# A fused attention, scan and MLP kernel: a chunk's normalisation chain queued later in stage 3, and half of an impulse response moved one step on

## The chip, the cores and the metric

The kernel runs on one core of a Trainium2 chip. The time is device microseconds of one execution, the median of three runs. A core has TensorE (PE), VectorE (DVE), ScalarE (ACT), GpSimd (POOL) and SyncE (SP), each with its own program; here SP issues all the DMA. The engines meet only at semaphores: an instruction waits until a semaphore has reached a count, and what stands behind it on its engine waits with it. All data are float32.

## The reference, cut to what matters

```python
# x: 128 batches x 32 tokens x 256;  ctx: 128 x 257 x 256
x = x + xattn(layernorm(x), ctx, w_sim, b_sim, W_qv, b_qv)

def attn(x, A, Bp, Cp, Dp, Wg, bg, gamma, beta):      # a gated linear scan over the 32 tokens
    xg = x * sigmoid(x @ Wg.T + bg)
    # s = s @ A + xt * Bp ;  y = s . Cp + Dp * xt   (per channel)
    y = scan(...) + xg
    return layernorm(y) * gamma + beta
x = x + attn(layernorm(x), ...)

def ffn(x, fast_b, w_fc, w_proj, u, v, gate):
    h = x @ (ternary(w_fc) * scale).T + gate * (x @ v.T @ fast_b.T @ u.T)
    r = maximum(h, 0)
    return (r * r) @ (ternary(w_proj) * scale).T      # hidden width 1024
x = x + ffn(layernorm(x), ...)
```

## The kernel before, in words

The 4096 tokens are 32 groups of 128. Stage 1 is a loop of 34 pipelined steps over the groups: in `step(g)` each engine works on the context of group g, the attention of g - 1 and the gate of g - 2. The scan is done as a convolution: every channel's impulse response over 32 tokens (`impulse`, from the state powers kept in `states`) is written to DRAM, read back as shifted windows, and placed in the matrix `toeplitz`, with which TensorE multiplies the gated tokens. The states are complete after step 28 (`LAST_STATE`); in step 29 GpSimd multiplies them by C, and VectorE sums them in two halves (`impulse_sums(0)`, `impulse_sums(1)`) and finishes with `impulse_response()`, which adds D and scales by 0.5. SP waits for that (`imp_steps`), stores the impulse, waits for the store and issues four loads of windows (`windows_load(q, 0)`); GpSimd and ScalarE place them from step 31 on.

In step 30 VectorE's order is: `bn_stats` of a coming group, x1 of group 28 (`resid` at L1500), the moments that `make_z` on ScalarE and `turn_z` on TensorE wait for, `normalise1(31)`, `hq`, `weights(30)` (a ternary pass), `dot1(31)` (L1413), then the products, `neg_max` and `zT_lo` (which TensorE's `sum_gate` waits for), and the softmax.

Stage 3 is the MLP over 8 chunks of 4 groups (512 tokens). A chunk c has 8 hidden tiles m. For each, TensorE makes `hidden_wide` (four matmuls, the high and low parts of xn against the ternary weights) and `hidden_low` (a fifth, the low-rank term), ScalarE a relu, VectorE the square, ScalarE its rounded high part `sq_hi`, GpSimd the rest `sq_lo`, and TensorE, three tiles behind, the projection: four matmuls with `sq_hi`, four with `sq_lo`. Two banks hold the hidden tiles, so a tile waits for the square two before it.

Before a chunk begins, its x must be made. With y the scan's output: sums and moments of y (`y_sums`, `y_moments`, DVE), the inverse deviation (`deviation_y`, `lower_y`, POOL), `norm_y` (ACT), `times_gamma` (POOL), `add_y` (DVE), and then the x chain: `x_sums`, `x_moments` (DVE), `deviation_x`, `lower_x` (POOL), `norm_x` (ACT), `turn_in` (PE transposes), `split_hi` (ACT), `split_lo` (DVE), `low_rank` (PE), `low_rank_hi` (ACT), `low_rank_parts` (DVE). Chunk 1 has a form of its own for the y part: `second_centre` and `second_add`, in halves. These steps are written by hand between the tiles of the chunks before: the loops over (c, m) of each engine say at which tile each step stands in that engine's queue. SP loads y of a chunk (`load_y`) when the adds before it are done (`x2_done`), which counts two for chunk 0 and one for each later chunk (`whole_chunks`).

## Time and profile before

| | us |
|---|---|
| three runs | 490.25, 490.37, 492.69 |
| median | 490.37 |
| profiled execution, its own time | 489.83 |
| its span, first to last instruction | 488.0 |
| PE busy | 467.5 (96%) |
| weight loads on PE | 403.8 (83%) |
| DVE busy | 398.0 (82%) |
| ACT busy | 361.5 (74%) |
| POOL busy | 340.3 (70%) |
| mean granted TensorE clock | 0.996 of full |

Stage 1 reaches to about 298 us of the span, the scan and the turning of the weights to about 326, and stage 3 from there to the end. A matmul's end is modelled and neighbours overlap, so a busy PE is not PE at its peak: from start to start is the better length. Idle time in brackets in a timeline is that of the engine ahead of the instruction, with what ended it. An engine that idles off the bound costs nothing.

### The profile page before, as it was taken

What the parts mean: (1) busy time and instruction counts of PE and PEld (TensorE: products, weight loads), DVE (VectorE), ACT (ScalarE), POOL (GpSimd) and SP (SyncE); (2) the same over time, 40 slices, a digit from 0 to 9 for tenths busy, and PEclk for the clock granted to TensorE, in tenths of its full rate; (3) what the DMA queues carried; (4) which work ended last, traced back from release to release, by engine and by line L of the source; (5) the groups of instructions that cost most, each with busy time, mean ns of one, the idle gap of its engine ahead of it and who ended that gap; (6) DMA issues with size and microseconds to landing.
All of it is one profiled execution on the core that took longest, in us unless ns stands there. A gap on an engine that the chain in (4) does not pass through costs nothing. (4 is left out here: it accounts for less than half of the span.)

```text
span 488.0 us, 13769 instructions
## 1 busy us (share of the span) xinstructions
PE 467.5 (96%) x4405; PEld 403.8 (83%) x4405; DVE 398.0 (82%) x1212; ACT 361.5 (74%) x880; POOL 340.3 (70%) x446
## 2 busy tenths in 40 slices
PE   8899999999999999999999898887999999999995
PEld 6688888989888898898988787776888888888885
DVE  2988888889889888899888876788769788797654
ACT  3787777878878878788787786656697786876752
POOL 2488997868667677776876766125789887887563
PEclk9999999999999999999999999999899999999999
DMA  7945647758757566674764747684021312301102
GB/s 258 316 151 161 217 155 195 223 155 241 184 148 229 145 194 186 164 218 140 230 171 142 192 120 164 144 259 130 0 57 32 87 43 45 87 6 39 44 1 88
DMA packets 77172, 70.29 MB, mean 144 GB/s; under 512 B 39319, under 2 KB 59948, under 8 KB 76588
## 3 DMA queue, kind: packets, MB, share of 16 engines
q1 hardware_dynamic: 77100, 69.41, 49.6%
q8 instruction: 36, 0.59, 0.5%
q14 instruction: 36, 0.29, 0.2%
HBM read 56.74 MB, written 12.65 MB: 142 GB/s over the span
## 5 line engine op out<-in xcount | busy, mean ns | idle before, releaser
L1958 POOL TENSOR_TENSOR sq_lo<-fc_in,sq_hi 128x512 fp32r<-128x512 f32 x63 | 82.7, 1315 | 29.3 <-ACT sq_hi L1909 29.3
L1041 ACT COPY ctxT<-turn_ps 128x512 f32<-128x512 f32 x128 | 68.9, 590 | 9.1 <-PE turn_ps L802 3.1
L1901 ACT ACTIVATE relu<-fc_ps,fc_square 128x512 f32<-128x512 f32 x64 | 43.8, 686 | 30.9 <-PE fc_ps L1820 30.8
L2003 DVE SCALAR_TENSOR_TENSOR fc_in<-fc_ps,relu 128x512 f32<-128x512 f32 x64 | 43.7, 685 | 26.4 <-ACT relu L1901 25.6
L1236 POOL TENSOR_TENSOR hb_lo<-hbT,hb_hi 128x256 fp32r<-128x256 f32 x32 | 23.9, 747 | 42.6 <-ACT hb_hi L1120 42.6
L1222 POOL TENSOR_TENSOR rstd<-ve,neg_half 128x1 f32<-128x1 f32 x64 | 35.1, 553 | 25.5 <-DVE ve L1511 18.4
L1814 PE MATMUL fc_ps<-xn_hi,fc_T 128*128 128x512 f32 x128 | 52.1, 407 | 0.5 <-DVE fc_in L2003 0.5
L1814 PE MATMUL fc_ps<-xn_lo,fc_T 128*128 128x512 f32 x128 | 50.9, 398 | 0.0
L1228 POOL TENSOR_TENSOR proj_in<-proj_in,below 128x512 f32<-128x512 f32 x31 | 48.1, 1552 | 0.0
L802 PE MATMUL turn_ps<-ident,ctxn 128*128 128x128 f32 x352 | 47.5, 278 | 0.0
L1837 PEld LDWEIGHTS proj_ps<-proj_T,sq_hi 128*128 128x128 f32 x252 | 38.8, 189 | 5.4
L1837 PE MATMUL proj_ps<-proj_T,sq_lo 128*128 128x256 f32 x252 | 40.2, 281 | 2.5 <-POOL sq_lo L1958 2.5
L802 PEld LDWEIGHTS turn_ps<-ident,ctxn 128*128 128x128 f32 x352 | 41.1, 147 | 0.4 <-ACT ctxT L1041 0.2
L1909 ACT CAST sq_hi<-fc_in 128x512 fp32r<-128x512 f32 x64 | 39.2, 613 | 1.9 <-DVE fc_in L2003 1.9
L1837 PE MATMUL proj_ps<-proj_T,sq_hi 128*128 128x256 f32 x252 | 40.3, 282 | 0.0
L1837 PEld LDWEIGHTS proj_ps<-proj_T,sq_lo 128*128 128x128 f32 x252 | 34.4, 188 | 2.7 <-POOL sq_lo L1958 2.7
L879 PE MATMUL score_ps<-ctxT,hcwT 128*32 128x257 f32 x512 | 33.7, 380 | 0.7 <-ACT ctxT L1041 0.7
L1814 PEld LDWEIGHTS fc_ps<-xn_hi,fc_T 128*128 128x128 f32 x128 | 24.3, 190 | 4.7 <-DVE fc_in L2003 1.3
L1048 ACT ACTIVATE xn<-resid,nmr,rstd 128x256 f32<-128x256 f32 x32 | 19.3, 603 | 11.0 <-DVE nmr L1456 10.8
L1072 ACT ACTIVATE hcwT<-hc_probT,w 128x128 f32<-128x128 f32 x62 | 27.3, 489 | 0.1
L1814 PEld LDWEIGHTS fc_ps<-xn_lo,fc_T 128*128 128x128 f32 x128 | 24.5, 191 | 3.3
L1236 POOL TENSOR_TENSOR hcq_lo<-y_in,hcq_hi 128x256 fp32r<-128x256 f32 x32 | 24.0, 751 | 4.0 <-ACT hcq_hi L1137 3.1
(261 smaller groups left out, 1449.5 us busy)
## 6 DMA issues: line engine op xcount, KB each, us to landing
ctxn<-in_ctx SPq DMA_DIRECT2D x22, 1024.0 KB, 5.5
toeplitz<-in_ctx SPq DMA_DIRECT2D x10, 1024.0 KB, 5.5
resid<-in_x SPq DMA_DIRECT2D x32, 128.0 KB, 5.4
ctx_end<-in_ctx SPq DMA_DIRECT2D x32, 128.0 KB
gated_tokens<-gated SPq DMA_DIRECT2D x32, 128.0 KB, 5.9
scan_x<-gated_tokens SPq DMA_DIRECT2D x60, 64.0 KB, 4.8
out<-resid SPq DMA_DIRECT2D x7, 512.0 KB, 3.2
scan_quarters<-scan_x SPq DMA_DIRECT2D x3, 1024.0 KB, 6.0
```

Source lines behind the costliest of these rows:

```text
L802: mm = pe.transpose(turn_ps[b % 2][:, (c * JT + t) * P:(c * JT + t + 1) * P], ctxn[g % DEEP][:, b, t, c * P:(c + 1) * P], ident[:, :])
L879: mm = pe.matmul(score_ps[b * L:(b + 1) * L, 0:J], hcwT[:, c, b * L:(b + 1) * L], ctxT[:, b, c, :], start=(c == 0), stop=(c == KD - 1))
L1041: act.copy(ctxT[:, b, :, 0:J - 1], turn_ps[b % 2][:, :].rearrange("p (k j) -> p k j", k=KD)).then_inc(ctxT_copied, 1)
L1222: pool.tensor_tensor(dst, src, neg_half[:, 0:1], ALU.pow).then_inc(made, 1)
L1228: pool.tensor_tensor(v_next[:, :, :, :], a_sb[:, :, :].rearrange("p k (n m) -> p k m n", n=N), state.unsqueeze(2).broadcast_to([P, KD, N, N]),
L1236: pool.tensor_tensor(lo, full, hi.bitcast(F32), ALU.subtract).then_inc(lo_ready, 1)
L1814: pe.matmul(fc_ps[m % 2][:, :], fc_T[:, k, m * P:(m + 1) * P], part[:, c % 2, k, :], start=(k == 0 and i == 0), stop=False)
L1837: mm = pe.matmul(proj_ps[c % 2][r // 2][:, (r % 2) * D:(r % 2 + 1) * D], part[:, tile(c, m) % PARTS, r * P:(r + 1) * P], proj_T[:, m, :], ...
L1901: act.activation(relu[m % 2], fc_ps[m % 2][:, :], ACT.Relu, scale=fc_square[:, m:m + 1]).then_inc(relu_done, 1)
L1909: act.copy(sq_hi[:, tile(c, m) % PARTS, :], sq[m % SQ]).then_inc(sq_hi_done, 1)
L1958: pool.tensor_tensor(sq_lo[:, tile(c, m) % PARTS, :], sq[m % SQ], sq_hi[:, tile(c, m) % PARTS, :].bitcast(F32), ALU.subtract).then_inc(sq_ ...
L2003: dve.scalar_tensor_tensor(out=sq[m % SQ], in0=fc_ps[m % 2][:, :], scalar=0.0, in1=relu[m % 2], op0=ALU.max, op1=ALU.mult).then_inc(sq_don ...
```

## The change

In stage 1, `impulse_sums(1)` and `impulse_response()` leave the end of VectorE's step 29 and stand in step 30 between `weights(30)` and `dot1(31)`. SP waits for the impulse after its own `step(29)` and no longer ahead of it.

In stage 3, chunk 1's steps stand later in the queues. The add of chunk 1 counts in halves (`summed_chunks`), its second half comes at tile 3 in place of 2, its sums are taken in halves (`second_sums`), and the moments follow at once. GpSimd meets `deviation_x(1)` at tile 4 in place of 2. ScalarE's `norm_x(1)` goes from tile 5 to 6, `split_hi(1)` from 6 to 7, `low_rank_hi(1)` from tile 7 of chunk 0 to tile 0 of chunk 1, with `norm_y(2)` behind it. TensorE turns chunk 1 behind hidden tile 7 in place of 5, and does `low_rank(1)` at the head of chunk 1. `add_y(2)` goes from tile 7 of chunk 0 to tile 0 of chunk 1. In chunk 1 the steps of chunk 2 and 3 on ScalarE, GpSimd and the turn on TensorE move one tile later. From chunk 2 on nothing is changed.

```diff
--- before.py
+++ after.py
@@ -305,8 +305,7 @@
             for r in half(h):
                 ins = dve.scalar_tensor_tensor(out=res(1, r), in0=y_second[:, r, :], scalar=rstd_y[:, r:r + 1],
                                                in1=res(1, r), op0=ALU.mult, op1=ALU.add)
-            if h == 1:
-                ins.then_inc(x2_done, 1)
+            ins.then_inc(x2_done, 1)
 
         def first_deviations(pool):
 
@@ -348,13 +347,26 @@
             part = resid[:, c * CH:(c + 1) * CH, :]
             dve.tensor_tensor(part, y_of(c)[:, :, :], part, ALU.add).then_inc(x2_done, 1)
 
+        def summed_chunks(n):
+
+            return n if n == 0 else (2 if n == 1 else n + 2)
+
         def x_sums(dve, c):
 
-            dve.wait_ge(x2_done, whole_chunks(c + 1))
+            dve.wait_ge(x2_done, summed_chunks(c + 1))
             at_least(dve, mv_x_done, whole_chunks(c))
             for r in range(CH):
                 ins = dve.bn_stats(bn_x[:, r, :], res(c, r))
             ins.then_inc(bn_x_done, 1)
+
+        def second_sums(dve, h):
+
+            dve.wait_ge(x2_done, 2 + h + 1)
+            at_least(dve, mv_x_done, whole_chunks(1))
+            for r in half(h):
+                ins = dve.bn_stats(bn_x[:, r, :], res(1, r))
+            if h == 1:
+                ins.then_inc(bn_x_done, 1)
 
         def x_moments(dve, c):
 
@@ -379,7 +391,7 @@
 
         def deviation_y(pool, c):
             pool.wait_ge(ve_y_done, whole_chunks(c + 1))
-            at_least(pool, x2_done, whole_chunks(min(c, 2)))
+            at_least(pool, x2_done, summed_chunks(min(c, 2)))
             at_least(pool, yn_done, 2 * (c - 2))
             pool.tensor_tensor(rstd_y[:, :], ve_y[:, :], neg_half[:, 0:CH], ALU.pow).then_inc(rstd_y_done, 1)
 
@@ -763,13 +775,13 @@
                     step(base, 0, ())
                     if base >= 4:
                         scan_load_pair(base)
+                    step(base + 1, 0, ())
                     if base + 1 == LAST_STATE + 1:
                         sp.wait_ge(imp_steps, IMPULSE)
                         sp.dma_start(impulse_dram.rearrange("(c p) l -> p c l", p=P), impulse[:, :, :]).then_inc(impulse_stored, 16)
                         sp.wait_ge(impulse_stored, 16)
                         for q in range(NB):
                             windows_load(q, 0)
-                    step(base + 1, 0, ())
 
                 for base in range(2, GROUPS - 2, 2):
                     body(base)
@@ -1558,6 +1570,9 @@
                     if g == GROUPS:
                         scaled_mean(g)
                     weights(g)
+                    if g == LAST_STATE + 2:
+                        impulse_sums(1)
+                        impulse_response()
                     if g + 1 < GROUPS:
                         dot1(g + 1)
                     if g == 1:
@@ -1637,9 +1652,6 @@
                         at_least(dve, pooled, g)
                         dve.tensor_scalar(pick[:, :], own_ps, top_e[:, 0:1], top_rec[:, 0:1],
                                           ALU.mult, ALU.mult).then_inc(pick_ready, 1)
-                    if g == LAST_STATE + 1:
-                        impulse_sums(1)
-                        impulse_response()
                     if g >= GROUPS:
                         gate(g - 2)
 
@@ -1722,7 +1734,7 @@
             def _(sp):
                 def load_y(c):
 
-                    at_least(sp, x2_done, whole_chunks(c - 1))
+                    at_least(sp, x2_done, summed_chunks(c - 1))
                     sp.wait_ge(y_stored[c // 2], 16)
                     y_load(sp, c)
 
@@ -1860,7 +1872,9 @@
                 low_rank(0)
                 for c in range(CHUNKS + 1):
                     for m in range(MT):
-                        if m == 7 and has(c, 1):
+                        if c == 1 and m == 0:
+                            low_rank(1)
+                        if m == 7 and c >= 1 and has(c, 1):
                             low_rank(c + 1)
                         if c == 0 and m == 0:
                             for i in range(2):
@@ -1871,6 +1885,8 @@
                         elif has(c) and (c, m) != (0, 1):
                             hidden_wide(c, m)
                             hidden_low(c, m)
+                        if c == 0 and m == 7:
+                            turn_in(1)
                         if m < BEHIND and has(c, -1):
                             if c == CHUNKS and m == BEHIND - 1:
                                 project_last(c - 1, MT - 1)
@@ -1878,7 +1894,7 @@
                                 project(c - 1, MT - BEHIND + m)
                         if m >= BEHIND and has(c):
                             project(c, m - BEHIND)
-                        if m == (5 if c == 0 else 4) and has(c, 1):
+                        if c >= 1 and m == (5 if c == 1 else 4) and has(c, 1):
                             turn_in(c + 1)
 
             @block.scalar
@@ -1921,17 +1937,18 @@
                 low_rank_hi(0)
                 for c in range(CHUNKS + 1):
                     for m in range(MT):
-                        if m == (6 if c == 0 else 5) and has(c, 1):
+                        if m == (7, 6, 5)[min(c, 2)] and has(c, 1):
                             split_hi(c + 1)
-                        if c == 0 and m == 5 or c == 1 and m == 3:
+                        if c == 0 and m == 6 or c == 1 and m == 4:
                             for h in range(2):
                                 norm_x(act, c + 1, h)
-                        if c == 0 and m == 6:
+                        if c == 1 and m == 0:
+                            low_rank_hi(1)
                             for h in range(2):
                                 norm_y(act, 2, h)
-                        if c == 1 and m == 4:
+                        if c == 1 and m == 5:
                             norm_y(act, 3, 0)
-                        if m == 7 and has(c, 1):
+                        if m == 7 and c >= 1 and has(c, 1):
                             low_rank_hi(c + 1)
                         if c == CHUNKS - 1 and m == MT - 1:
                             square_hi(c, m - 1)
@@ -1943,7 +1960,7 @@
                             scan_copy(act, PIECES * BLOCKS - 1, scan_bank(PIECES * BLOCKS - 1))
                         if m == 0 and has(c, -1):
                             square_hi(c - 1, MT - 1)
-                        if c == 1 and m == 4:
+                        if c == 1 and m == 5:
                             norm_y(act, 3, 1)
                         if c >= 2 and m in (2, 3) and has(c, 1):
                             norm_x(act, c + 1, m - 2)
@@ -1963,15 +1980,15 @@
                 deviation_y(pool, 1)
                 for c in range(CHUNKS):
                     for m in range(MT):
-                        if c == 0 and m == 5:
+                        if c == 0 and m == 7:
                             for h in range(2):
                                 times_gamma(pool, 2, h)
                         if c == 1 and m in (4, 5):
                             times_gamma(pool, 3, m - 4)
-                        if m == (2, 1, 0, 1)[min(c, 3)] and has(c, 1):
+                        if m == (4, 2, 0, 1)[min(c, 3)] and has(c, 1):
                             deviation_x(pool, c + 1)
                             lower_x(pool, c + 1)
-                        if m == (4 if c == 0 else 2) and has(c, 2):
+                        if m == (5, 3, 2)[min(c, 2)] and has(c, 2):
                             deviation_y(pool, c + 2)
                             lower_y(pool, c + 2)
                         if c >= 2 and m in (4, 6) and has(c, 2):
@@ -2036,20 +2053,17 @@
                 second_centre(dve, 0)
                 for c in range(CHUNKS + 1):
                     for m in range(MT):
-                        if m == (6 if c == 0 else 5) and has(c, 1):
+                        if m == (7, 6, 5)[min(c, 2)] and has(c, 1):
                             split_lo(c + 1)
-                        if m == 7 and has(c, 1):
+                        if m == 7 and c >= 1 and has(c, 1):
                             low_rank_parts(c + 1)
                         if c == 0:
-                            if m == 4:
-                                x_moments(dve, 1)
-                            if m == 5:
+                            if m == 6:
                                 y_sums(dve, 2, half(1))
                                 y_moments(dve, 2)
                         if c == 1:
-                            if m == 1:
-                                x_sums(dve, 2)
-                                x_moments(dve, 2)
+                            if m == 0:
+                                low_rank_parts(1)
                             if m == 7:
                                 add_y(dve, 3)
                         if has(c):
@@ -2057,19 +2071,25 @@
                         if c == 0:
                             if m == 0:
                                 second_centre(dve, 1)
-                            if m in (1, 2):
-                                second_add(dve, m - 1)
+                            if m == 1:
+                                second_add(dve, 0)
+                            if m == 2:
+                                second_sums(dve, 0)
                             if m == 3:
-                                x_sums(dve, 1)
+                                second_add(dve, 1)
+                                second_sums(dve, 1)
+                                x_moments(dve, 1)
                             if m == 4:
                                 y_sums(dve, 2, half(0))
-                            if m in (5, 6):
-                                y_sums(dve, 3, half(m - 5))
-                            if m == 7:
-                                add_y(dve, 2)
+                            if m in (6, 7):
+                                y_sums(dve, 3, half(m - 6))
                         if c == 1:
                             if m == 0:
                                 y_moments(dve, 3)
+                                add_y(dve, 2)
+                            if m == 1:
+                                x_sums(dve, 2)
+                                x_moments(dve, 2)
                             if m == 7:
                                 x_sums(dve, 3)
                         if c == 2 and m == 0:
```

## Rows read from the trace of the kernel before

**Rows 1.** Windows: us, PE, PEld, DVE, ACT, POOL busy (instructions), PEclk, DMA share, GB/s

```profile
335.00:340.00 5.00, 2.49 (x16) 2.05 (x15) 4.53 (x19) 2.35 (x6) 2.95 (x5) 1.00 0.46 105
...
340.50:341.00 0.50, 0.41 (x3) 0.41 (x4) 0.00 (x0) 0.50 (x2) 0.50 (x2) 0.79 0.00 0
...
344.00:344.50 0.50, 0.50 (x4) 0.46 (x3) 0.50 (x2) 0.50 (x3) 0.00 (x0) 0.79 0.00 0
```

**Rows 2.** Timeline, stage 3, chunk 0: start us, length us, engine, line, operation [idle before]

```profile
336.98 1.01 POOL L389 TENSOR_TENSOR rstd_x<-ve_x,neg_half 128x4 f32<-128x4 f32 x1 [3.29 <-DVE ve_x L369]
...
338.46 2.07 ACT L375 ACTIVATE xn<-resid,shift_x,rstd_x 128x256 f32<-128x256 f32 x4 [2.65 <-POOL shift_x L397]
...
339.70 0.73 PE L1837 MATMUL proj_ps<-proj_T,sq_lo 128*128 128x256 f32 x4 [2.51 <-POOL sq_lo L1958]
```

**Rows 3.** Timeline, adds on VectorE that meet GpSimd's `sq_lo`

```profile
332.81 1.55 DVE L306 SCALAR_TENSOR_TENSOR resid<-below,rstd_y,resid 128x256 f32<-128x256 f32 x2
...
348.79 1.29 POOL L1958 TENSOR_TENSOR sq_lo<-fc_in,sq_hi 128x512 fp32r<-128x512 f32 x1 [0.40 <-ACT sq_hi L1909]
348.85 2.31 DVE L349 TENSOR_TENSOR resid<-y_in,resid 128x1024 f32<-128x1024 f32 x1
```

**Rows 4.** Chain of waits, chunk 1: start us, length us, engine, tile, line

```profile
357.39 0.92 PE fc_ps L1814 x4
358.54 0.96 PE proj_ps L1837 x8
359.51 0.87 PE xt_ps L1795 x8
```

**Rows 5.** Timeline, the hand-off from the turned xn to the low-rank parts, and y

```profile
342.45 1.07 ACT L1889 CAST xn_hi<-xt_ps 128x512 fp32r<-128x512 f32 x2 [0.83 <-PE xt_ps L1795]
...
343.41 2.08 ACT L334 ACTIVATE y_in<-y_in,shift_y,rstd_y 128x256 f32<-128x256 f32 x4
...
343.56 1.29 DVE L1987 TENSOR_TENSOR xn_lo<-xt_ps,xn_hi 128x512 fp32r<-128x512 f32 x2 [1.06 <-ACT xn_hi L1889]
...
344.58 2.55 POOL L342 TENSOR_TENSOR y_in<-y_in,gamma_all 128x512 f32<-128x512 f32 x2 [0.95 <-ACT y_in L334]
...
346.47 0.59 ACT L1895 CAST lr_hi<-xt_ps 128x512 fp32r<-128x512 f32 x1
...
347.36 0.73 DVE L1995 SCALAR_TENSOR_TENSOR lr_parts<-lr_hi,minus_lo,xt_ps 128x512 fp32r<-128x512 f32 x1
```

**Rows 6.** Timeline, chunk 1, the chain of chunk 2

```profile
352.26 1.39 DVE L356 BATCH_NORM_STATS2 bn_x<-resid 128x6 f32<-128x256 f32 x4
...
355.91 2.08 ACT L375 ACTIVATE xn<-resid,shift_x,rstd_x 128x256 f32<-128x256 f32 x4 [0.32 <-POOL shift_x L397]
...
362.05 1.05 ACT L1889 CAST xn_hi<-xt_ps 128x512 fp32r<-128x512 f32 x2
...
364.57 0.47 PE L1804 MATMUL xt_ps<-xn_hi,low_in 128*128 128x512 f32 x1
```

**Rows 7.** Timeline, TensorE ahead of chunk 0

```profile
324.86 0.47 PE L1804 MATMUL xt_ps<-xn_hi,low_in 128*128 128x512 f32 x1 [1.53 <-DVE xn_lo L2031]
```

**Rows 8.** Window of the impulse's second half: us, DVE busy (instructions), PEclk, DMA share, GB/s

```profile
271.10:272.45 1.35, 1.20 (x3) 1.00 0.76 132
```

**Rows 9.** Timeline, steps 30 and 31 of stage 1

```profile
274.59 1.73 SPq L760 DMA_DIRECT2D proj_in<-impulse  x4
...
276.05 0.44 PE L886 MATMUL gate_ps<-ident,xn 128*128 128x128 f32 x2 [1.08 <-ACT xn L1048]
...
277.30 0.41 DVE L1413 SCALAR_TENSOR_TENSOR y_in<-hc,att_ps 128x256 f32<-128x256 f32 x1
...
278.86 0.48 PE L894 MATMUL gate_ps<-wgT_hi,zT_hi 128*128 128x256 f32 x2 [0.25 <-DVE zT_lo L1588]
...
286.06 1.03 POOL L1265 COPY toeplitz<-proj_in 32x1024 f32<-32x1024 f32 x1
```

**Rows 10.** DMA issues: KB each, median us from issue to landing

```profile
proj_in<-impulse SPq DMA_DIRECT2D x4, 240.0 KB, 4.7
```

## The prediction

> **What bounds the kernel now.** I read the busy shares by stretch first, then the timeline of the stretch that stood out, then the chain of waits behind it. TensorE is the busy engine all along; of the five-microsecond stretches of stage 3 one is half empty, 2.49 of 5.00 us [rows 1]. In the timeline [rows 2] the hole is one wait: TensorE's `sq_lo` half of a projection starts at 339.70 after 2.51 us of idling for GpSimd. GpSimd had been put to `deviation_x(1)` ahead of `square_lo(0, 2)`, and that one (336.98) was waiting for VectorE's moments of chunk 1. Then the granted clock falls: 0.79 in the half microsecond from 340.50 and again 0.79 in the one from 344.00, 0.50 between, so about 3.5 us at 1.2 GHz [rows 1]; on work that keeps TensorE full this is 1.75 us lost. After it the chain of waits is TensorE's own work, tile by tile [rows 4]. The stall and the slow clock are together 2.51 + 1.75 = 4.3 us: that is all that the first rearrangement has to win. The other one touches the end of stage 1, where TensorE has two small waits in group 30: 1.08 us before `turn_z` and 0.25 us before `sum_gate` [rows 9].
>
> **Part 1, chunk 0 of stage 3: the lead that TensorE gets.** The change adds no arithmetic. It sends the chunk's x chain through the queues later, and GpSimd meets `deviation_x(1)` two squares later. I follow the new order with durations of before.
> - VectorE still does, before `ve_x(1)`, the second add, four sums, the moments and square 3. The same instructions end at the same time, but for one: the second add (two instructions, 1.55 us beside a GpSimd `sq_lo` [rows 3]) now meets `square_lo(0, 2)`, which is no longer held. It may wait a little longer or not at all: 0 to +0.7 us (a whole such operation less the overlap); I take +0.15. The activations of `norm_x(1)`, 338.46 to 340.53 [rows 2], become 338.6 to 340.7.
> - TensorE: without the wait the `sq_lo` half starts at 339.70 - 2.51 = 337.2. From there, at full clock, half a projection 0.48, hidden 6 (0.92 for four matmuls and a fifth, 1.15 from start to start), projection 3 (0.96), hidden 7 (1.15) [rows 4]: 340.9, and 0.1 for the wait on square 4. `turn_in(1)` finds xn ready (340.7) and takes 0.87: 341.9. Projection 4: 342.85.
> - Now the hand-off is bare. After the turn come ScalarE's split 1.07, VectorE's split 1.29 and two hand-overs of 0.05 [rows 5]: 344.4. TensorE idles 342.85 to 344.4, 1.5 us. `low_rank(1)` (four matmuls, 0.93) ends at 345.3. `hidden_low(1, 0)` waits for `lr_hi` 0.59 and `lr_parts` 0.73 [rows 5] and two hand-overs: 346.8, a further 0.5 us of idling, and it ends at 347.0.
> - Before, the same work from 339.70 on is, at full clock, 0.48 + 0.87 + 0.93 + 3 x 1.15 + 2 x 0.96 = 7.65 us, plus 1.75 for the slow clock and 0.16 of waiting: 349.3. So the lead at this point is 2.3 us.
>
> **Part 1, chunk 1: who gives it back.** `norm_y(2)` and its gamma moved behind `low_rank_hi(1)`, and the chain from there carries chunk 2.
> - `lr_hi(1)` ends at 345.3 + 0.05 + 0.59 = 345.95. Gamma's first half starts 1.17 us after the start of `norm_y` (344.58 less 343.41) and both halves take 2.55 [rows 5]: 347.1 to 349.65.
> - GpSimd goes on at once with `square_lo(0, 7)`, whose `sq_hi` is there: four activations 2.08, a relu and a cast of about 0.6 each, 349.2. `add_y(2)` then starts a few hundredths behind it. The trace has just this pair: GpSimd's at 348.79, the add at 348.85 taking 2.31 us, that is 1.29 of GpSimd and its own 1.0 [rows 3]. So `add_y(2)` ends at 352.0, square (1, 1) at 352.6, and `x_sums(2)` starts at 352.6, where it started at 352.26 [rows 6]: 0.35 us later than before, though TensorE is over 2 us ahead.
> - From there to `low_rank(2)` the order on ScalarE is the same work: `norm_x(2)` four activations, then relu, cast, half of `norm_y(3)`, twice, then the split. Before: sums 352.26, norm 355.91, split 362.05, `low_rank(2)` 364.57 [rows 6], without idling on ScalarE between the last three. Shifted: norm 356.25, split 362.4, VectorE's split to 364.8, `low_rank(2)` 364.9.
> - TensorE alone would have been there long before: from 347.0, projections 0.96 and hidden tiles 1.15 (six of each, and a seventh projection), one turn 0.87 and some 0.9 us of waits for squares behind `add_y` and `x_sums` make about 362.4. It idles 2.2 to 2.6 us in front of `low_rank(2)`.
> - Sum of part 1: 364.9 less 364.57, +0.3 us. Bounds: -0.1 (the add uncontended in chunk 0, hand-overs all short) to +0.7. From chunk 2 on the queues are as before and TensorE fills them [rows 4], so what it is late by there stays, perhaps less a tenth or two: I take +0.2.
>
> The row on the add beside GpSimd has a rule behind it. The Trainium skill's page "SBUF — State Buffer", section "Who interferes with whom", says that a VectorE instruction with two SBUF inputs and a GpSimd instruction reading SBUF exclude each other, and that the one issued first holds the port while the other waits in full. By that rule, the trace agrees (2.31 us against 1.29 + 1.0). It also says that nothing but the order decides, which is the second rival below.
>
> **Part 2, the impulse.** It removes three VectorE instructions (1.20 us busy, 1.25 of the queue [rows 8]) from the end of step 29 and puts them between `weights(30)` and `dot1(31)`. Between the two places VectorE runs nearly without a hole, so the first half of step 30 comes 1.25 us earlier: `make_z` and with it `turn_z` no longer wait, and TensorE's 1.08 us [rows 9] go. But `dot1(31)` starts at 277.30 [rows 9] both ways, since the same instructions stand before it. All behind it, `zT_lo` among them, has its old time, and TensorE starts `sum_gate` at 278.86 [rows 9] as before: it now waits 0.25 + 1.08 = 1.3 us there, with 0.4 more that stood as issue time. Sum: 0. Bounds: -1.1, if `zT_lo` moves up after all, to +0.3.
> SP: the impulse is ready at 277.2 in place of 272.5, behind step 29's two transfers. The windows were issued at 274.59 over 1.73 us and took 4.7 to land [rows 9, 10]; they go 4.8 us later, 279.4 to 281.1, and land by 285.8. GpSimd places them from 286.06 [rows 9]. The cover is 0.3 us, and behind it `hcq_lo` has some 0.7 us until TensorE needs it. Gone, each microsecond beyond 1 costs one; taken at 0.
>
> **Sum.** The profiled execution took 489.83 us, the median of the runs is 490.37. +0.2 and 0 on the median: 490.6 us.
>
> **Rivals.**
> - A, slower: the clock falls at the new gap. Before, TensorE idled 2.51 us and 0.16 us more shortly after, and the clock fell [rows 1, 2]; a gap of 1.53 us at 323.3 left it at full, the matmul after it taking 0.47 us [rows 7]. The new gap of 2.2 to 2.6 us before `low_rank(2)` lies between, near the first. What follows it is TensorE-bound, so 3.5 us at 1.2 GHz cost 1.75 less a little that the ScalarE chain hides: +1.5, 492.1. It decides from a gap somewhere above 1.5 us. The gap of 1.5 before `low_rank(1)` is a weaker candidate, and its cost would lie inside the lead. Chance 0.25.
> - B, faster by less: `add_y(2)` gets ahead of `square_lo(0, 7)`, or `zT_lo` moves up in stage 1. The first needs `sq_hi(0, 7)` later than gamma's end; I have it 0.45 us earlier. It brings 1.2 us on the chain of chunk 2, of which TensorE's own arrival leaves all: 489.5. The second brings 1.1: 489.5 too. Chance 0.13.
> - C, faster: the chain of chunk 2 does not bind (ScalarE and VectorE keep pace with TensorE) and the 2.3 us of lead stay: 488.3; with the bare hand-off also covered, 4.3 us: 486.3. For it speaks that the visible stall and the slow clock really go; against it the sum above. Chance 0.14, of which 0.09 beyond 0.5%.
> - D: the windows land over 1 us late, or VectorE's longer queue delays the squares of chunk 0: 493 and more. Chance 0.08.
> - E: the wait on `sq_lo(0, 2)` moves to `sq_lo(0, 4)` and stays as long: 490 plus the bare hand-off, 493. GpSimd would have to be held at `deviation_x(1)` to 339; by the sum it is held 0.1 us. Within D's chance.
>
> **How the numbers follow.** The forecast has 0.40, at 490.0 to 491.3. What a measurement here can tell from no change is 0.5%, 2.45 us: under 487.9 is faster, over 492.8 slower. Faster: C's far part, 0.10. Slower: D, and A where the clock falls at both places or costs its full 1.75 on top of +0.7: 0.13. Same: 0.77. For 8 in 10 the range takes A's and B's centres and stops inside C: 488.4 to 492.8.
>
> **What would show it.** `PE L1837 <- POOL sq_lo` near 337 gone, and full clock from 337 to 345; a wait of about 1.5 us before `low_rank(1)` and of over 2 us before `low_rank(2)`, both on `xn_lo`; `x_sums(2)` starting within half a microsecond of 352.3, behind an `add_y` of 2.3 us; in group 30 the wait before `turn_z` gone and one of 1.3 to 1.7 us before `sum_gate`. Wrong if `x_sums(2)` starts before 351, if `low_rank(2)` finds its input ready, or if `sum_gate` in group 30 starts clearly before 278.8.

## The result, and the profile after

The changed kernel took 495.50 us (median of 6 runs, 492.94 to 496.19), the kernel before 491.45 beside it on the same chip: 1.0082 of its time, interval 1.0060 to 1.0103. A second series gave 494.05 against 490.91, 1.0068 (1.0044 to 1.0093). By these ratios it is slower by 3.3 to 4 us, where 490.6 and "no difference" had been forecast, and it lies above the range of 488.4 to 492.8. The profiled execution took 492.94 us with a span of 491.2; the one of before took 489.83 with 488.0. The 3.2 us between the spans are what I account for first.

TensorE's own landmarks cut the span: the first matmul of `sum_gate` in steps 29, 30 and 32 of stage 1 (that of step 31 lies between, at 289.74 after and 287.33 before), then those of `low_rank(0)`, `(1)` and `(2)` in stage 3. Each distance below is the difference of two such start times in the timelines (after: 268.97, 279.75, 297.52, 327.05, 347.07, 367.75; before: 268.36, 278.86, 295.11, 324.86, 345.24, 364.57).

```
us                      to g29   g29-g30  g30-g32  g32-LR0  LR0-LR1  LR1-LR2  LR2-end
before                  268.36   10.50    16.25    29.75    20.38    19.33    123.43
after                   268.97   10.78    17.77    29.53    20.02    20.68    123.45
difference               +0.61   +0.28    +1.52    -0.22    -0.36    +1.35     +0.02
after, second series    269.42   10.79    17.80    29.54    20.00    20.69
```

The first 0.61 lies ahead of everything that was edited and scatters from execution to execution: step 29 is at 267.84 to 269.42 in the profiles of this study. The -0.22 from step 32 to `low_rank(0)` is in no edited stretch either: that one took 29.53 to 30.99 us where the clock was full, and up to 31.70 where it fell. The impulse's part costs 1.80, stage 3 costs 0.99 net. In stage 3 only the sum from `low_rank(0)` to `low_rank(2)` compares like with like, because the new order does hidden tile 7 and projection 4 of chunk 0 ahead of `low_rank(1)` and the old one behind it. The second series agrees within 0.04 in every edited stretch.

**Stage 3.** The stall is gone and the clock stays at full where it had fallen. These are windows of the changed kernel from the place of [rows 1] to `low_rank(1)`, and one around `low_rank(2)` (us, then PE, PEld, DVE, ACT and POOL busy with instructions, granted clock, DMA share, GB/s):

```profile
335.00:340.00 5.00, 4.86 (x32) 4.19 (x30) 4.90 (x15) 2.79 (x5) 3.97 (x4) 1.00 0.41 140
340.00:345.00 5.00, 4.94 (x32) 4.45 (x33) 3.79 (x14) 4.26 (x8) 4.31 (x8) 1.00 0.31 69
345.00:350.00 5.00, 2.85 (x13) 1.95 (x12) 3.31 (x7) 3.42 (x8) 1.87 (x3) 1.00 0.00 0
...
366.00:371.00 5.00, 3.25 (x18) 2.87 (x19) 3.31 (x5) 2.85 (x6) 2.64 (x3) 1.00 0.61 128
```

The hole moved: the stretch that was half empty is full, the one around `low_rank(1)` is busy for 2.85 of 5 us in its place, and the one around `low_rank(2)` is a third empty. In TensorE's timeline the waits of chunks 0 and 1 answer to the 2.51 and 0.16 of before:

```profile
347.07 0.47 PE L1816 MATMUL xt_ps<-xn_hi,low_in 128*128 128x512 f32 x1 [1.63 <-DVE xn_lo L2004]
...
349.69 0.50 PE L1832 MATMUL fc_ps<-lr_parts,low_out 128*128 128x512 f32 x1 [0.52 <-DVE lr_parts L2012]
...
367.75 0.47 PE L1816 MATMUL xt_ps<-xn_hi,low_in 128*128 128x512 f32 x1 [2.10 <-DVE xn_lo L2004]
```

1.63, 0.52 and 2.10 were forecast as 1.5, 0.5 and 2.2 to 2.6. What is behind them, in the timeline of VectorE, GpSimd and ScalarE, is the answer to [rows 3, 5, 6]:

```profile
340.98 2.08 ACT L387 ACTIVATE xn<-resid,shift_x,rstd_x 128x256 f32<-128x256 f32 x4 [0.33 <-POOL shift_x L409]
...
342.36 0.17 DVE L246 TENSOR_SCALAR ve_y<-mv_y 128x4 f32<-128x4 f32 x1
...
348.27 0.59 ACT L1911 CAST lr_hi<-xt_ps 128x512 fp32r<-128x512 f32 x1 [1.58 <-PE xt_ps L1816]
...
352.43 3.60 POOL L1975 TENSOR_TENSOR sq_lo<-fc_in,sq_hi 128x512 fp32r<-128x512 f32 x2
352.45 1.30 DVE L246 TENSOR_SCALAR ve_y<-mv_y 128x4 f32<-128x4 f32 x1
353.67 1.21 DVE L348 TENSOR_TENSOR resid<-y_in,resid 128x1024 f32<-128x1024 f32 x1
...
355.40 1.39 DVE L359 BATCH_NORM_STATS2 bn_x<-resid 128x6 f32<-128x256 f32 x4
```

Read the two `ve_y` rows: the same instruction on 128x4 numbers takes 0.17 us alone and 1.30 us when GpSimd started a `sq_lo` 0.02 us before it. The add behind it then starts just ahead of GpSimd's second `sq_lo` and takes 1.21, where I had it wait (2.31); here it is the `sq_lo` that waits, and takes 2.34 us in place of 1.30 (the two are merged in the row of 3.60).

**Stage 1.** The wait of 1.08 before `turn_z` [rows 9] is gone, and one wait of 1.78 stands before `sum_gate`; right behind it the granted clock is at half for 3.4 us. TensorE's timeline of the changed kernel, and its windows:

```profile
279.75 0.47 PE L906 MATMUL gate_ps<-wgT_hi,zT_hi 128*128 128x256 f32 x2 [1.78 <-DVE zT_lo L1603]
```

```profile
280.00:281.00 1.00, 1.00 (x9) 1.00 (x9) 0.91 (x5) 0.88 (x6) 1.00 (x2) 0.77 0.00 0
281.00:282.00 1.00, 1.00 (x7) 1.00 (x7) 0.87 (x4) 1.00 (x4) 1.00 (x2) 0.50 0.19 67
282.00:283.00 1.00, 1.00 (x6) 1.00 (x6) 0.00 (x0) 0.50 (x2) 0.45 (x2) 0.50 0.70 213
283.00:284.00 1.00, 1.00 (x7) 1.00 (x6) 0.65 (x2) 0.00 (x0) 0.62 (x1) 0.52 1.07 267
```

On VectorE, GpSimd and SP, the rows that answer to [rows 8, 9]:

```profile
277.29 0.73 POOL L1266 TENSOR_TENSOR resid<-resid,beta_all 128x256 f32<-128x256 f32 x1
277.36 0.67 DVE L1459 SCALAR_TENSOR_TENSOR impulse_sb<-d_sb,impulse_sb 128x2 f32<-128x2 f32 x1
...
278.29 0.38 SPq L781 DMA_DIRECT2D impulse<-impulse_sb  x1
...
280.65 1.74 SPq L772 DMA_DIRECT2D proj_in<-impulse  x4
```

### The profile page after: what moved, and what is told of

Same layout as the page of the kernel before. It is cut to its first block and busy times, and to the rows that moved or that the text cites. A ratio compares the mean times of both kernels' runs of the same rounds, so it can differ in the third digit from the quotient of the medians.

```text
span 491.2 us, 13770 instructions
## 1 busy us (share of the span) xinstructions
PE 468.3 (95%) x4405; PEld 404.3 (82%) x4405; DVE 397.9 (81%) x1212; ACT 361.7 (74%) x880; POOL 341.1 (69%) x446
## 5 line engine op out<-in xcount | busy, mean ns | idle before, releaser
L814 PEld LDWEIGHTS turn_ps<-ident,ctxn 128*128 128x128 f32 x352 | 42.1, 150 | 0.4
L1145 ACT CAST hq_hi<-feat_ps 128x256 fp32r<-128x256 f32 x32 | 11.9, 373 | 20.4 <-DVE y_in L1586 20.4
```

What stands on the lines that cost most here:

```text
L814: mm = pe.transpose(turn_ps[b % 2][:, (c * JT + t) * P:(c * JT + t + 1) * P], ctxn[g % DEEP][:, b, t, c * P:(c + 1) * P], ident[:, :])
```

## The experiments

My theory for stage 3 was that late input decides (a chain over VectorE, GpSimd and ScalarE), the rival that the falls of the clock do; for the impulse's part, late windows against the clock. Differences between two experiments are of their means, with a 95% interval by resampling their executions. All were timed in five rounds beside the kernel before. Comparisons of b_sp with b_only, of y_first, y_early and a_fill with a_only, and of y_late with y_early are between two series, and the mean of the kernel before moved by 0.1 to 0.3 us from one series to the other; "LR0-LR1" and the like are the distances of the table above in the profiled execution.

**The changed kernel again (after_again).** No edit.

> The changed kernel once more. Its profiled execution took 492.94 us, five others 494.1 to 496.2: something is spread over executions. Theory (clock): the new gaps of TensorE (1.78 us before sum_gate of step 30, 1.63 before low_rank(1), 2.10 before low_rank(2)) are each followed by 3.5 us at 1.2 GHz in some executions, so this profile shows either one fall as before (493 us) or two (495 to 496 us), the second behind one of the stage 3 gaps. Rival (constant cost): all executions have the same stalls and the spread is in stage 1 or in the transfers; then two profiles differ outside these places. Ratio to the kernel before 1.008.

Measured: 494.05 us, ratio 1.0068 (1.0044 to 1.0093); one fall of the clock in the profile, behind `sum_gate` at the same place (281.4 to 284.8).

**Each part alone.** The stage 3 edits without the impulse's (a_only), and the impulse's move without the others (b_only). First a_only:

> The stage 3 part alone; stage 1 as before. Theory (clock + chain): low_rank(2) comes 1.0 us later after low_rank(0) than before (40.7 for 39.7 us), as in the changed kernel, plus 1.5 in executions where the clock falls behind a stage 3 gap: +1 to +2.5 us, ratio 1.002 to 1.005. Rival (my forecast): +0.2, ratio 1.000 to 1.001. Rival (stage 3 innocent): the whole loss is in stage 1, ratio 1.000 or below.

Measured: 493.0 us, 1.0036 (1.0014 to 1.0057). LR0-LR1 20.00, LR1-LR2 20.69, the same as in the full change. Here the clock fell behind the gap of 2.10 before `low_rank(2)`, with the distance from there to `low_rank(3)` (LR2-LR3) at 20.37 instead of 18.82. It also fell for about as long at 313, in a stretch that no edit touches, behind a gap of 1.84. The windows behind the first gap:

```profile
368.00:369.00 1.00, 1.00 (x4) 0.81 (x3) 0.00 (x0) 0.46 (x1) 0.00 (x0) 0.50 0.01 2
369.00:370.00 1.00, 1.00 (x3) 0.72 (x3) 0.84 (x2) 0.12 (x1) 0.00 (x0) 0.50 0.00 0
```

Then b_only:

> The impulse's move alone. Theory (clock): TensorE's wait before sum_gate of step 30 is 1.7 us in place of 0.25, the clock falls behind it and stays at half for 3.4 us, steps 30 and 31 are 1.8 us longer together: +1.8 to +2, ratio 1.004. Rival (my forecast): the stalls only change place, +0, ratio 1.000. Rival (transfers): the windows land later and GpSimd waits for them: seen as GpSimd idle before the placing copies in step 31.

Measured: 492.37 us, 1.0024 (1.0002 to 1.0047). The clock didn't fall in this profile, neither behind the wait of 1.81 at `sum_gate` nor behind the old stall. And the time is still lost: g29-g30 10.80, g30-g32 17.31. The chain of waits says where (start us, length us, what):

```profile
277.22 0.21 DVE impulse_sb L1450
277.43 0.02 issue
277.44 2.33 DMA impulse<-impulse_sb
279.77 0.02 issue
279.79 0.31 SPq L760
...
281.09 6.46 DMA proj_in<-impulse
...
287.70 0.02 POOL toeplitz L1265
...
289.51 0.74 POOL hcq_lo L1236
290.25 0.04 issue
290.29 0.52 PE qv_ps L815 x2
```

From the impulse's last operation to a matmul of step 31 it is one unbroken chain: store, windows, placing on GpSimd, `hcq_lo` queued behind it, TensorE. The fourth window load lands 6.46 us after its issue. My 4.7 [rows 10] was the median of the four; of before's own four the slowest took 5.7. In TensorE's timeline the chain ends in a wait of 0.83, most of the 1.06 that g30-g32 is longer. How late the windows are differs between executions. From `sum_gate` of step 30 to the first placing on GpSimd it is 7.20 us in before, and 7.51 (b_sp), 8.06 (b_fill2), 8.41 (b_fill), 8.75 (after_fill) and 8.80 (b_only) with the move; g30-g32 is 16.25, and then 16.24, 16.60, 16.94, 17.24 and 17.31. So being late by up to about 0.5 us costs nothing, and each microsecond beyond it costs one.

This profile also has the old stage 3 without a fall of the clock: LR0-LR1 19.41, LR1-LR2 19.43, together 38.84 instead of before's 39.71.

**The impulse's move with the gap filled (b_fill).** 12 idle transposes, that is of the identity, into a free bank, with a result that nothing reads:

```diff
+                    if g == LAST_STATE + 2:
+                        for i in range(12):
+                            pe.transpose(turn_ps[0][:, 0:P], ident[:, :], ident[:, :])
                     if has_c:
                         sum_gate(g - 2)
```

> The impulse's move alone, and TensorE does 12 transposes of the identity into a free bank ahead of sum_gate of step 30 (1.3 us of work in the 1.8 us gap; extra work that nothing reads). Theory (clock): with TensorE busy the clock stays at 2.4 GHz and the cost of b_only goes: step 30 is 10.5 us as before, ratio 0.999 to 1.001. Rival (VectorE's queue): the cost is in zT_lo and what follows on VectorE, not in the clock; then b_fill is as slow as b_only, 1.004.

Measured: 491.69 us, 1.0013 (0.9993 to 1.0033); mean 0.45 below the move alone, between -1.55 and +0.68, so not resolved. The mean clock rose from 0.9932 to 0.9959. The late windows stayed (g30-g32 16.94).

**The impulse's move with SP's order as it was (b_sp).** The store and the windows again ahead of `step(31)`'s loads, VectorE's part still moved.

> The impulse move alone, with SP's store and windows ahead of the loads of step 31, where they stood before. Theory L (the windows land late: GpSimd waits 1.70 us for them and TensorE 0.83 for GpSimd): the windows are issued 0.5 to 1 us earlier, TensorE's wait on hcq_lo goes, 0.3 to 0.8 us faster than the impulse move alone. Rival: SP holds the loads of step 31 for the impulse, and these are then what the step waits for: the same or slower.

Measured: 492.0 us, 1.0024 (1.0004 to 1.0044), no gain in time over the move alone (-0.16, -1.3 to +1.0). In the profile the mechanism is right: windows issued at 279.58 on a step 29 that is 0.5 later, so 0.7 earlier against it, GpSimd's wait down from 1.70 to 0.37, and g30-g32 at 16.24, the value of the kernel before. g29-g30 keeps its +0.29. That the median doesn't show the 1.06 is a miss of theory L's number, and its cause stays open: the falls of the clock were as frequent as in the move alone (mean clock 0.9934 and 0.9932).

**Stage 3: `add_y(2)` ahead of `y_moments(3)` (y_first).**

```diff
-                                y_moments(dve, 3)
                                 add_y(dve, 2)
+                                y_moments(dve, 3)
```

> The stage 3 part alone, with add_y(2) ahead of y_moments(3) in chunk 1. Theory P (the chain of chunk 2 is late because y_moments(3) sat in front of add_y(2): its small tensor_scalar took 1.30 us beside GpSimd's sq_lo): x_sums(2) starts 0.5 to 0.9 us earlier against low_rank(0) than in the stage 3 part alone, low_rank(0) to low_rank(2) falls from 40.7 to about 40.0, and the time by 0.5 to 0.9 us. Rival Q (the port is held either way; add_y(2) meets the two sq_lo itself and takes 2.3 us or more in place of 1.2): x_sums(2) moves by less than 0.3 us and the time doesn't change.

Measured: 494.84 us, 1.0086 (1.0060 to 1.0112); 2.1 (1.0 to 3.2) slower than the stage 3 part alone. LR1-LR2 21.77, 1.08 more, and behind `low_rank(2)` the clock fell (LR2-LR3 20.36). Theory P fell: both instructions now wait, each for its own `sq_lo`, as rival Q had it for the add; but Q's "the time doesn't change" missed too. VectorE's timeline:

```profile
350.14 2.30 DVE L348 TENSOR_TENSOR resid<-y_in,resid 128x1024 f32<-128x1024 f32 x1 [0.37 <-POOL y_in L341]
...
352.76 0.84 DVE L246 TENSOR_SCALAR ve_y<-mv_y 128x4 f32<-128x4 f32 x1
```

**Stage 3: `norm_y(2)`'s first half where ScalarE idles (y_early).**

```diff
                             low_rank_hi(1)
-                            for h in range(2):
-                                norm_y(act, 2, h)
+                            norm_y(act, 2, 1)
...
+                        if c == 0 and m == 7:
+                            norm_y(act, 2, 0)
```

> The stage 3 part alone, with the first half of norm_y(2) in the 1.6 us in which ScalarE idles before low_rank_hi(1). Theory P (TensorE's gap before low_rank(2) is the chain norm_y(2), gamma, add_y(2), sums, norm_x(2), split): gamma starts about 2 us and ends about 1.3 us earlier, x_sums(2) too, the wait before low_rank(2) falls from 2.1 to 1.0 us or less, low_rank(0) to low_rank(2) from 40.7 to 39.4 to 39.8, time 1.0 to 1.5 us below the stage 3 part alone. Rival R (the loss of that part is the clock falling at new gaps, the chain isn't what binds): low_rank(0) to low_rank(2) stays above 40.3.

Measured: 492.04 us, 1.0026 (1.0008 to 1.0044), 0.8 below the stage 3 part alone (-1.75 to +0.24), not resolved. LR1-LR2 20.23: 0.46 won of the 0.9 to 1.3 expected. `x_sums(2)` does start 0.92 earlier against `low_rank(1)` (7.41 us behind it, in place of 8.33). Half of that is lost again at the next small instruction, `ve_x(2)`, which took 0.28 at the end of a `sq_lo` and now meets one that has 0.72 us left:

```profile
355.08 0.75 DVE L381 TENSOR_SCALAR ve_x<-mv_x 128x4 f32<-128x4 f32 x1
```

**The same, with `y_moments(3)` behind `x_moments(2)` (y_late).**

```diff
                             if m == 0:
-                                y_moments(dve, 3)
                                 add_y(dve, 2)
...
+                            if m == 2:
+                                y_moments(dve, 3)
```

> The stage 3 part alone, with the first half of norm_y(2) ahead of low_rank_hi(1), and y_moments(3) out of the chain of chunk 2: on VectorE behind x_moments(2). Theory P (after low_rank(1) everything up to low_rank(2) is one chain over VectorE and ScalarE, and each thing taken out of it brings low_rank(2) nearer): x_sums(2) starts about 1.2 us earlier after low_rank(1) than with norm_y(2) early alone (7.4 us), low_rank(1) to low_rank(2) falls from 20.2 to 19.0 to 19.4 us, the wait before low_rank(2) to 1 us, the time by 0.8 to 1.2. Rival Q (add_y(2) then meets GpSimd's sq_lo itself, 2.3 us in place of 1.2): 20.2 stays.

Measured: 492.70 us, 1.0021 (1.0000 to 1.0043); LR1-LR2 20.22, as rival Q had it: out of `ve_y`'s way, `add_y(2)` met the `sq_lo` itself. The time isn't resolved from that of the version before (+0.4, -0.7 to +1.4). The wait before `low_rank(2)` was to fall to 1 us in both; it stayed at 2.09 and 2.10, and was 2.08 in y_first where `low_rank(2)` came 1.08 later. Its length doesn't measure what the chain costs.

```profile
351.59 2.33 DVE L348 TENSOR_TENSOR resid<-y_in,resid 128x1024 f32<-128x1024 f32 x1
...
356.28 0.80 DVE L381 TENSOR_SCALAR ve_x<-mv_x 128x4 f32<-128x4 f32 x1
```

**Filling the gaps of the stage 3 part.** 12 idle transposes before `low_rank(1)`, 16 before `low_rank(2)` (a_fill); the same on y_late, with 5 in place of 16 (y_late_fill). First a_fill:

> The stage 3 part alone, with 12 idle transposes in TensorE's gap before low_rank(1) and 16 in the one before low_rank(2). Theory P (the loss is late input, the clock only adds some executions' falls): the waits shrink by what the transposes take, low_rank(0) to low_rank(2) stays at 40.7, the median moves by -0.7 to +0.2 us. Rival R (the loss is the clock): 1.5 us or more faster than the stage 3 part alone, level with the kernel before or below.

Measured: 492.29 us, 1.0024 (1.0007 to 1.0041), 0.67 less than the part alone (-1.6 to +0.3), not resolved. The waits shrink to 0.30 and 0.34, LR0-LR1 stays 19.99 and LR1-LR2 20.65: TensorE isn't late, its input is.

Then y_late_fill:

> The same with idle transposes in TensorE's gaps before low_rank(1) (12) and before low_rank(2) (5). If the falls of the clock at these gaps are worth what the earlier fillings showed (0.7 us each), 0.3 to 0.8 us below the kernel without them, that is 490.3 to 491: level with the kernel before. If the time still lies over 491.5, something in stage 3 is lost that neither the chain nor the clock explains.

Measured: 490.94 us, 0.9999 (0.9983 to 1.0014), 1.2 (0.3 to 2.1) less than without the transposes. Here the clock's share is resolved: its mean is 0.9987 in place of 0.9952, with no execution under 0.997. The profiled execution has the same distances as `y_late` up to `low_rank(2)`, to 0.01, and behind it 18.80 in place of 20.35, where the clock had fallen.

**The changed kernel with all three gaps filled (after_fill).**

> The changed kernel, with idle transposes in its three new gaps: 12 before sum_gate in step 30, 12 before low_rank(1), 16 before low_rank(2). Theory P with the clock beside it: the waits as far as they are late input stay (low_rank(0) to low_rank(2) 40.7), the clock stays at full near 281 to 285 and 368 to 371: 492.5 to 493.3, some 1.5 us below the changed kernel and 2 to 2.5 above the kernel before. Rival R (the whole loss is the clock): 490.5 to 491.

Measured: 493.09 us (8 runs), 1.0051 (1.0025 to 1.0078); distances 10.81, 17.24, 19.99, 20.69, no fall of the clock anywhere in the profiled execution (mean over all eight 0.9971). So 2.5 us of the loss are there with these falls prevented, and rival R falls. The mean lies 3.3 us (2.2 to 4.6) above those of the two versions of the kernel before with filled gaps, further down, though these were timed in other series; in the profiles the edited stretches differ by 0.30 + 1.01 + 1.84 = 3.15 us from those of before_fill.

**The kernel before with its stall filled (before_fill).** 18 idle transposes:

```diff
                         if i == 1:
+                            if tile(c, m) == 2:
+                                pe.wait_ge(scan_copied, PIECES * BLOCKS)
+                                for j in range(18):
+                                    pe.transpose(proj_ps[1][0][:, 0:P], ident[:, :], ident[:, :])
                             at_least(pe, sq_lo_done, tile(c, m) + 1)
```

> The kernel before, with 18 idle transposes inside its 2.5 us stall before the sq_lo half of projection (0, 2). If the stall is what the clock falls on: no execution with a fall there, low_rank(0) to low_rank(2) at 38.8 instead of 39.7, median 0.3 to 0.9 us faster. Rival: the fall is no matter of that gap: the same time, and the clock still low near 340 to 344 in the profile.

Measured: 489.95 us, 0.9984 (0.9967 to 1.0001). The clock is full through 340 to 345, and LR0-LR2 is 38.84, as in b_only, where the clock stayed up at this stall without any filling. In b_sp, with the same stage 3, it fell, and the distance was 39.77. The windows at the place of [rows 1]:

```profile
340.00:345.00 5.00, 3.94 (x25) 3.35 (x26) 3.02 (x6) 4.90 (x11) 4.63 (x7) 1.00 0.00 0
```

It is the fastest version of the study, though its interval just reaches no difference.

**Two fillings, without and with the impulse's move.** Six more transposes at the end of stage 2 (before_fill2); the second kernel has the move and its 12 as well (b_fill2).

> The kernel before, with 18 idle transposes in its 2.5 us stall before the sq_lo half of projection (0, 2) and 6 at the end of stage 2, ahead of TensorE's gap of 1.5 us or more near 312. If the falls of the clock behind these two gaps make the spread of this kernel's time: granted clock of 0.996 or more in most executions, median 489.0 to 489.9, 0.7 to 1.6 us below the kernel before, a spread under 2 us. If the time is not a matter of these falls: the same as with the first filling alone, 489.9 to 490.3, and falls in the records as often as there.

Measured: 490.23 us, 0.9987 (0.9971 to 1.0003). The clock was 0.997 or more in 11 of 12 executions, but the time is no better than with one filling, and 0.4 us below the kernel before where 0.7 to 1.6 were expected: the spread of this kernel's time isn't only its clock.

> The same two fillings, the impulse move, and 12 idle transposes before sum_gate in step 30. The difference to the kernel with the fillings alone is what the impulse move costs with the clock left out: theory L (late windows, wait on hcq_lo 0.46, and TensorE's wait at sum_gate in place of turn_z): +0.4 to +0.9 us. Rival (its cost is only the fall of the clock behind sum_gate): -0.2 to +0.3.

Measured: 491.55 us, 1.0018 (1.0001 to 1.0035). Against the kernel with the fillings alone, 1.25 us (0.5 to 2.0) slower: the impulse's move costs time. The rival is excluded, and most of L's 0.4 to 0.9 is in the interval. Some of the 1.25 is still clock: four of the twelve executions had a mean clock under 0.995, one of the other kernel's. Among those at 0.997 or more the difference is 0.9 (0.3 to 1.4). The profile has +0.25 and +0.36 in its two distances.

## Why the prediction was wrong

What failed in part 1 is the prize, stall plus slow clock, 4.3 us, out of which the lead was taken. What failed in part 2 are three terms put at nothing: that `dot1(31)` starts at its old time, that the windows land in time, and that the clock stays up at the gap before `sum_gate`.

**Part 2 was the larger miss: 0 forecast, 1.8 us measured in both profiles of the change, and 0.6 to 1.4 where the clock didn't fall and SP's order was changed too.** Three terms:
- "`dot1(31)` starts at 277.30 [rows 9] both ways." The three impulse operations took 1.54 us in place of 1.28. (The 1.20 of [rows 8] is too small: its window ends inside the third of them.) L1459 took 0.67 in place of 0.40, beside an add that GpSimd had begun 0.07 us before it. It ended with that add (278.03, the add at 278.02), and so it had before (272.29, GpSimd's operation at 272.27): the 0.40 that I carried over was itself a shorter wait. `zT_lo` and `sum_gate` came 0.28 later, in all seven profiles with the move (10.78 to 10.81, against 10.50 to 10.55 in the nine without). My bound was +0.3.
- "They go 4.8 us later, 279.4 to 281.1, and land by 285.8." In b_only they were issued 279.79 to 281.1 and the last landed at 287.6. I took the median latency where the slowest of four decides. That one took 5.7 to 6.0 us in the profiles without the move, and 4.9 to 6.5 with it. "Gone, each microsecond beyond 1 costs one" was right but for the 1, which is about 0.5: 0.36 to 1.06 lost in g30-g32. This was rival D, at 0.08.
- The gap of 1.78 at `sum_gate`. I had counted it (1.3 + 0.4) and weighed the clock only for the gaps of stage 3. In both profiles of the changed kernel the clock fell there, at a cost of 1.5 in g30-g32, which then also covers the late windows (GpSimd found them landed at 288.48). With the gap filled and the clock full (after_fill) the late windows still cost 0.99, so the fall adds only about 0.5 to them. In b_only and b_sp, behind waits of 1.81 and 1.80, it didn't.

**Part 1: +0.3 forecast, +1.0 measured against the profile before, and that basis was wrong.**
- The waits came where they were put: `x_sums(2)` 8.33 us behind `low_rank(1)` against 8.2, `low_rank(2)` 12.35 behind that against 12.3. That the 8.2 fits is luck: the add took 1.21 and not 2.31, and `ve_y`, which the sum doesn't have, took 1.30.
- The 344.4 for `low_rank(1)` is 19.54 behind `low_rank(0)`; it was 19.99 to 20.02 in all nine profiles of the new order. Of the 0.48, 0.18 is `norm_x(1)` (0.33 later than before, taken at 0.15), the rest the way from there through turn and splits, 6.09 where I had 5.8.
- "The stall and the slow clock are together 2.51 + 1.75 = 4.3 us: that is all that the first rearrangement has to win." The slow clock was that execution's: [rows 1] show a fall that b_only and b_fill, with the same stage 3, don't have, and where it happened it cost 0.87 in the chain (0.93 in b_sp), not 1.75. Nor could the stall give back its 2.51: between `low_rank(0)` and `(2)` the old order without a fall takes 38.84 us, 1.0 more than two chunks of the steady state (18.92 each, from `low_rank(2)` to `(3)` in before). That this is about what was left to win is my reading; no run had the stall taken out and the chains kept. Against an execution without the fall, my own 364.9 was already a loss of 1.2 us, and the measured one is 1.86. The lead went the same way: at `hidden_low(1, 0)` it was put at 2.3 us, and was 1.70 against the profile before (22.64 behind `low_rank(0)` against 24.34) and 0.82 against b_only's (23.46).
- Rival A (the clock falls at the gap before `low_rank(2)`) was real in some executions (a_only, y_first, y_late), absent in both profiles of the full change. "It decides from a gap somewhere above 1.5 us" doesn't hold as a rule: the clock fell behind 1.63, 1.78, 1.84, 2.10 and 2.52, and not behind 1.72, 1.81, 2.10 and 2.53 in other executions.

The sum of the two parts with the clock left out is 0.28 + 0.36 to 1.06 + 1.86 = 2.5 to 3.2 us, against 3.3 and 4.0 measured for the whole, and 1.8 + 1.2 for the parts timed alone.

What the port rule says more: the Trainium skill's page "SBUF — State Buffer", section "Who interferes with whom", names `tensor_scalar` among the VectorE operations that can take the pair shared with GpSimd, when their operands meet further conditions, beside the adds that I cited it for. By that rule, the trace agrees (1.30, 0.85, 0.75 and 0.80 us for a 128x4 operation that takes 0.17 alone). Whether the operation meets the page's conditions, no run here shows. I had applied the rule to the large add only, and in each of the three attempts to mend the chain the wait moved to another instruction.

**What stays open**: why b_sp doesn't gain in time what its profile gains, what makes the clock fall in one execution and not in the next, and the 1.5 to 2 us by which executions of one kernel differ at the same clock. The distances say at least where the last lies: the start of step 29 moves by 1.6 us between profiles and the stretch from step 32 to `low_rank(0)` by 1.5 at full clock, both unedited, while from `low_rank(2)` to the end all profiles without a fall lie between 123.31 and 123.50.

## What to carry to other kernels

A stall in one execution's profile is worth what the chain behind it leaves: measure from landmark to landmark, in several profiles, before calling stall plus slow clock the prize. Where several transfers are waited for together, take the slowest, not the median, and where they are early by only 0.3 us, put a price on their coming late. Beside a busy GpSimd a small VectorE operation can take as long as GpSimd's (1.30 us here, in place of 0.17): on a chain, count the meetings, not the sizes.

## What the runs showed of the hardware that was not expected

- Whether the clock falls behind a gap of 1.8 to 2.5 us differs between executions of the same code: it fell behind the old stall in before and b_sp, and not in b_only. For the kernel before the mean granted clock ran from 0.990 to 0.998. Idle transposes in the gap kept it at full (y_late_fill, 0.9987).
- A fall of 3.4 us at half clock cost 0.87 us on a chain that TensorE doesn't bind alone (39.71 against 38.84), and 1.55 us where it does (LR2-LR3 20.37 against 18.82).
- Four DMAs of one kind, issued over 1.7 us, landed after 3.5 to 6.5 us each (b_only).
- Of a GpSimd and a VectorE operation that meet, the one that came second waits: `sq_lo` beside `add_y(2)` took 2.34 us in place of 1.30 where the add had started first, and the add 2.30 in place of 1.21 where `sq_lo` had.
